# Four-chunk slabs in a LayerNorm pass, K weights loaded in pieces, and residual loads on another queue

## The reference

```python
xn = _layernorm(x)                       # mean and variance over 4096 features
qkv = einsum('bsd,od->bso', xn, w_qkv)   # 32 query heads, 8 key/value heads of 128
q, k = rope(q), rope(k)
attn = softmax(where(causal, q @ k.T / sqrt(128), min)) @ v
attn_out = einsum('bso,do->bsd', attn, w_o)
ffn_out = xn @ kernel + bias + lora_delta(xn) + shared_lora_delta(xn)
return x + attn_out + ffn_out
```

## Time and profile before

| | us |
|---|---|
| median of two timed runs | 6041.11 (5918.13 to 6164.09) |
| profiled execution, timed | 5750.58 |
| its span on the slowest core (core 7) | 5749.0 |
| spans of the other cores | 5671.9 to 5723.1 |
| PE busy / DVE / ACT / POOL on core 7 | 4163.0 / 1117.4 / 977.1 / 556.1 |

### The profile page before, as it was taken

How to read it: one execution, slowest core, us unless ns; L and a number is a source line. 1 busy time by engine, 2 the same in 40 slices (tenths; PEclk the granted TensorE clock), 3 DMA queues, 4 the chain that set the end, 5 groups by cost and what they waited for, 6 DMA issues and landing times.

```text
span 5749.0 us, 44972 instructions; the slowest of 8 cores (5671.9 to 5749.0 us)
## 1 busy us (share of the span) xinstructions
PE 4163.0 (72%) x16144; PEld 1520.2 (26%) x16144; DVE 1117.4 (19%) x1874; ACT 977.1 (17%) x1041; POOL 556.1 (10%) x866
## 2 busy tenths in 40 slices
PE   2233399769959996767777777777775999557788
PEld 0000144334424441111111111111111444223333
DVE  0444322201102221111111111111111110011122
ACT  2232000000000003333333333333332000000000
POOL 0000000000000001111111111111111000010110
PEclk9666699889979998888888888888887999778899
DMA  9666332353256650010000000000003553465543
GB/s 141 121 123 119 105 106 77 85 120 103 82 101 92 94 77 28 27 30 26 26 26 26 28 26 27 26 26 26 26 27 57 96 93 62 92 121 127 126 102 96
DMA packets 412761, 419.81 MB, mean 73 GB/s; under 512 B 63360, under 2 KB 374912, under 8 KB 412160
## 3 DMA queue, kind: packets, MB, share of 16 engines
q0 software_dynamic: 219712, 249.10, 24.6%
q1 hardware_dynamic: 192832, 167.82, 9.5%
HBM read 495.46 MB, written 83.89 MB: 101 GB/s over the span
## 4 chain that ended last, share of the span: by engine, by line
PE 64%; DMA 11%; ACT 8%; DVE 8%; another core or an unknown queue 6%; issue 3%; POOL 0%; DVEq 0%; ACTq 0%; SPq 0%; POOLq 0%
PE kv_p L86 15%; PE a_rw L81 10%; PE a_av L86 9%; ACT a_p L81 8%; PE w_p L86 8%; PE q_p L86 7%; PE f_p L86 7%; DMA sc_xkv<-lkv_o 6%; DVE a_rc L81 4%; DMA f_at<-sc_at 3%; PE a_s L86 2%; PE a_s L81 2%; DVE lkv_o L81 1%; PE f_pl L86 1%
## 5 line engine op out<-in xcount | busy, mean ns | idle before, releaser
L81 ACT ACTIVATE a_p<-a_s,p_btab 128x1024 bf16<-128x1024 f32 x768 | 814.7, 1111 | 2982.1 <-PE a_s L81 2982.0
L86 PE MATMUL a_av<-a_p,a_v 128*128 128x512 bf16 x1536 | 644.2, 419 | 417.9 <-ACT a_p L81 299.9
L81 PE MATMUL a_rw<-a_p,p_onesb 128*1 128x512 bf16 x1536 | 627.9, 409 | 0.0
L86 PE MATMUL f_p<-f_k,f_x 128*128 128x512 bf16 x2048 | 472.9, 391 | 162.4 <-DVE f_s L81 111.6
L86 PE MATMUL kv_p<-kv_w,kv_x 128*128 128x512 bf16 x1984 | 441.1, 380 | 83.3 <-DMA kv_w<-wvT 83.3
L86 PE MATMUL q_p<-q_x,q_w 128*128 128x512 bf16 x1984 | 440.6, 380 | 71.8 <-DMA q_x<-sc_xkv 71.8
L86 PE MATMUL kv_p<-kv_x,kv_w 128*128 128x512 bf16 x1984 | 440.0, 380 | 69.2 <-DMA kv_x<-sc_xkv 69.2
L86 PE MATMUL w_p<-w_w,p_attn 128*128 128x512 bf16 x1984 | 441.5, 381 | 39.1 <-DMA w_w<-woT 39.1
L81 DVE TENSOR_TENSOR a_p<-a_p,p_cm 128x512 bf16<-128x512 bf16 x256 | 97.5, 422 | 1687.2 <-ACT a_p L81 1687.2
L86 PEld LDWEIGHTS a_av<-a_p,a_v 128*128 128x128 bf16 x1536 | 148.6, 97 | 911.4 <-issue 911.4
L86 PE MATMUL a_s<-a_q,a_k 128*128 128x512 bf16 x768 | 317.3, 413 | 12.8 <-DMA a_k<-sc_k 12.8
(11 more groups left out here) (93 smaller groups left out, 2182.0 us busy)
## 6 DMA issues: line engine op xcount, KB each, us to landing
kv_x<-sc_xkv SPq DMA_DIRECT2D x16, 4096.0 KB, 17.6
lkv_x<-xTkv POOLq DMA_DIRECT2D x8, 4096.0 KB, 37.3
sc_xkv<-lkv_o SPq DMA_DIRECT2D x256, 128.0 KB, 1.9
q_w<-wqT POOLq DMA_DIRECT2D x16, 2048.0 KB, 16.4
w_w<-woT POOLq DMA_DIRECT2D x8, 4096.0 KB, 26.1
f_k<-kern POOLq DMA_DIRECT2D x8, 4096.0 KB, 26.1
a_k<-sc_k POOLq DMA_DIRECT2D x384, 64.0 KB, 2.1
a_v<-sc_v POOLq DMA_DIRECT2D x192, 128.0 KB, 2.7
```

Of the source, the lines that this page charges most:

```text
L81: getattr(eng, m)(*aa, **kk).then_inc(s, st)
L86: getattr(eng, m)(*aa, **kk)
```

## The change

Four edits. In `ln_pass` the squares, the additions and the multiplications work on slabs of four groups (128x2048) instead of single groups, and one store writes a slab (512 KB); in the statistics loop the sum matmuls of a slab are now issued after the wait for its square. The mean and reciprocal rows are given to VectorE as an operand repeated four times. The buffers `lkv_q`, `lkv_t` and `lkv_o` grow fourfold. The K weights are issued in eight pieces of 1 MB by a hook that `ln_pass` calls once in each chunk, right behind the load of the next chunk. In `final_phase` the loads of `f_xc` and `f_at` move from the `gd` queue to the `sy` queue.

```diff
--- before.py
+++ after.py
@@ -206,14 +206,15 @@
     def fview(t):
         return t.rearrange("(a p) t -> p a t", p=128)
 
-    def ln_pass(xT_in, ntok, sc_out, tag):
+    def ln_pass(xT_in, ntok, sc_out, tag, hook=None):
         nch = ntok // CH
+        SLAB = 4 * CH
         with ExitStack() as ps:
             pp = ps.enter_context
             xch = [pp(nc.sbuf_tensor(f"l{tag}_x{i}", [128, 32 * CH], BF16)) for i in range(2)]
-            sq = [pp(nc.sbuf_tensor(f"l{tag}_q{i}", [128, CH], BF16)) for i in range(2)]
-            tb = [pp(nc.sbuf_tensor(f"l{tag}_t{i}", [128, CH], BF16)) for i in range(2)]
-            ob = [pp(nc.sbuf_tensor(f"l{tag}_o{i}", [128, CH], BF16)) for i in range(2)]
+            sq = [pp(nc.sbuf_tensor(f"l{tag}_q{i}", [128, SLAB], BF16)) for i in range(2)]
+            tb = [pp(nc.sbuf_tensor(f"l{tag}_t{i}", [128, SLAB], BF16)) for i in range(2)]
+            ob = [pp(nc.sbuf_tensor(f"l{tag}_o{i}", [128, SLAB], BF16)) for i in range(2)]
             srow = pp(nc.sbuf_tensor(f"l{tag}_s", [1, CH], F32))
             qrow = pp(nc.sbuf_tensor(f"l{tag}_ss", [1, CH], F32))
             mrow = pp(nc.sbuf_tensor(f"l{tag}_m", [1, CH], F32))
@@ -232,7 +233,6 @@
             tdep = [0, 0]
             odep = [None, None]
             row_done = 0
-            pe_stats_done = 0
             gd.wait(s_ve, xfree[0])
             xload[0] = gd.dma(out=xch[0][:].rearrange("p (a t) -> p a t", a=32),
                               in_=fview(xT_in)[:, :, 0:CH])
@@ -244,19 +244,25 @@
                     xload[ni] = gd.dma(
                         out=xch[ni][:].rearrange("p (a t) -> p a t", a=32),
                         in_=fview(xT_in)[:, :, (tc + 1) * CH:(tc + 2) * CH])
+                if hook is not None:
+                    hook(tc)
                 pe.waitd(xload[xi])
                 pe.wait(s_ve, row_done)
-                for dc in range(32):
-                    si = dc % 2
-                    xt = xch[xi][:, dc * CH:(dc + 1) * CH]
-                    pe.call("matmul", p_sum[0:1, :], sb_onesb[:, 0:1], xt,
-                            start=(dc == 0), stop=(dc == 31))
+                for sl in range(8):
+                    si = sl % 2
                     ac.waitd(xload[xi])
                     ac.wait(s_pe, qdep[si])
-                    av = ac.call("activation", sq[si][:], xt, AF.Square)
+                    av = ac.call("activation", sq[si][:],
+                                 xch[xi][:, sl * SLAB:(sl + 1) * SLAB], AF.Square)
                     pe.wait(s_ac, av)
-                    pq = pe.call("matmul", p_sq[0:1, :], sb_onesb[:, 0:1], sq[si][:],
-                                 start=(dc == 0), stop=(dc == 31))
+                    for k in range(4):
+                        dc = 4 * sl + k
+                        pe.call("matmul", p_sum[0:1, :], sb_onesb[:, 0:1],
+                                xch[xi][:, dc * CH:(dc + 1) * CH],
+                                start=(dc == 0), stop=(dc == 31))
+                        pq = pe.call("matmul", p_sq[0:1, :], sb_onesb[:, 0:1],
+                                     sq[si][:, k * CH:(k + 1) * CH],
+                                     start=(dc == 0), stop=(dc == 31))
                     qdep[si] = pq
                 pe_stats_done = pe.ctr.v
                 ve.wait(s_pe, pe_stats_done)
@@ -291,21 +297,27 @@
                 ve.call("tensor_copy", bcm[:], p_bc[:, 0:CH])
                 bcv = ve.call("tensor_copy", bcr[:], p_bc[:, CH:2 * CH])
                 ve.wait(s_ve, bcv)
+                bcm_b = bcm[:].unsqueeze(1).broadcast_to((128, 4, CH))
+                bcr_b = bcr[:].unsqueeze(1).broadcast_to((128, 4, CH))
                 last_tt = 0
-                for dc in range(32):
-                    ti = dc % 2
+                for sl in range(8):
+                    ti = sl % 2
                     ve.wait(s_ve, tdep[ti])
-                    v1 = ve.call("tensor_add", tb[ti][:],
-                                 xch[xi][:, dc * CH:(dc + 1) * CH], bcm[:])
+                    xs = xch[xi][:, sl * SLAB:(sl + 1) * SLAB]
+                    v1 = ve.call("tensor_add",
+                                 tb[ti][:].rearrange("p (a t) -> p a t", a=4),
+                                 xs.rearrange("p (a t) -> p a t", a=4), bcm_b)
                     ve.waitd(odep[ti])
                     ve.wait(s_ve, v1)
-                    v2 = ve.call("tensor_mul", ob[ti][:], tb[ti][:], bcr[:])
+                    v2 = ve.call("tensor_mul",
+                                 ob[ti][:].rearrange("p (a t) -> p a t", a=4),
+                                 tb[ti][:].rearrange("p (a t) -> p a t", a=4), bcr_b)
                     tdep[ti] = v2
                     last_tt = v2
                     sy.wait(s_ve, v2)
                     odep[ti] = sy.dma(
-                        out=sc_out[dc * 128:(dc + 1) * 128, tc * CH:(tc + 1) * CH],
-                        in_=ob[ti][:])
+                        out=fview(sc_out)[:, 4 * sl:4 * sl + 4, tc * CH:(tc + 1) * CH],
+                        in_=ob[ti][:].rearrange("p (a t) -> p a t", a=4))
                 xfree[xi] = last_tt
 
     def rope_block(b0, b1, cs, sn, bufs, dst0, dst1):
@@ -430,12 +442,15 @@
         kv_sinb = plk(nc.sbuf_tensor("kv_sin", [128, S], BF16))
         wk_deps = [gd.dma(out=kv_cosb[:], in_=i_cos_kv),
                    gd.dma(out=kv_sinb[:], in_=i_sin_kv)]
-        for piece in range(4):
-            wk_deps.append(gd.dma(
-                out=wsb[:].rearrange("p (a o) -> p a o", a=32)[
-                    :, piece * 8:(piece + 1) * 8, :],
-                in_=fview(i_wkT)[:, piece * 8:(piece + 1) * 8, :]))
-        ln_pass(i_xTkv, S, sc_xkv, "kv")
+
+        def wk_hook(tc):
+            if tc < 8:
+                wk_deps.append(gd.dma(
+                    out=wsb[:].rearrange("p (a o) -> p a o", a=32)[
+                        :, tc * 4:(tc + 1) * 4, :],
+                    in_=fview(i_wkT)[:, tc * 4:(tc + 1) * 4, :]))
+
+        ln_pass(i_xTkv, S, sc_xkv, "kv", hook=wk_hook)
         barrier()
         kv_sweeps(wsb, kv_cosb, kv_sinb, wk_deps)
     barrier()
@@ -798,16 +813,16 @@
                 xcv = None
                 for tt in range(8):
                     if tt % 4 == 0:
-                        gd.wait(s_ve, xcdep)
-                        xcv = gd.dma(out=xc[:].rearrange("p (a t) -> p a t", a=4),
+                        sy.wait(s_ve, xcdep)
+                        xcv = sy.dma(out=xc[:].rearrange("p (a t) -> p a t", a=4),
                                      in_=i_xown.rearrange("(a p) d -> p a d", p=128)[
                                          :, tt // 4 * 4:tt // 4 * 4 + 4,
                                          oc * CH:(oc + 1) * CH])
                     par = tt % 2
                     pb = pf[par]
                     api = tt % 2
-                    gd.wait(s_ve, atdep[api])
-                    av_ = gd.dma(out=at[api][:],
+                    sy.wait(s_ve, atdep[api])
+                    av_ = sy.dma(out=at[api][:],
                                  in_=sc_at[tt * 128:(tt + 1) * 128,
                                            oc * CH:(oc + 1) * CH])
                     pe.waitd(kv_[ki])
```

## The result

| | before | changed |
|---|---|---|
| median of the timed runs, us | 5901.5 (10 runs) | 5479.51 (11 runs) |
| lowest, us | 5767.34 | 5456.22 |
| ratio | 1 | 0.9478, interval 0.9457 to 0.950 |

The change makes the kernel 5.2% faster; of 5768 us that is 301 us, against 296 forecast.

The account below looks back on a forecast made before the run. It saw a LayerNorm pass waiting on two chunk buffers and stores, and a last phase held by sc_at loads behind kern; 176 + 120 = 296 us off the 6041 us median gave 5745, range 5450 to 5900.

Parts of the forecast that it names:

- (a): Start of LayerNorm pass: K weights behind x let x0 land at about 62 us instead of 103, 41 us saved.
- The sum of 107 us for two chunks: LayerNorm pass, per buffer: load 41, statistics 20, rows 9.3, normalising 37 us, so 54 us a chunk.
- (b): LayerNorm statistics: eight slab squares instead of 32 take 20 us a chunk instead of 21, bounds 17 and 29.
- (c): LayerNorm normalising: 16 slab operations of at most 1.36 us, 35 to 40 us a chunk beside a load.
- The pair beside a load: LayerNorm normalising: two 512 KB stores during an x load take 8 to 16 us, 12 taken.
- Rival 1: LayerNorm pass: stores starve by turns during loads, chunk 61 us, 260 us saved in all, 5781 us; chance 0.17.
- (d): Last phase: sc_at and xown loads on the sync queue save 18.3 us in six blocks, 10 in the first, together 120.
- tile 2 is then free of the kern load: Last phase, block head: after 1 to 2 us lost at tile 1, kern no longer delays tile 2's load.
- as now: Last phase, tile 4 of a block: the xown load there was expected to behave as before the change.
- the 2.6 us and the landing: Last phase, SP's queue: 2.6 us before a tile's load is issued, plus its landing time T, against 8.2 a tile.
- the 19.9 us lost per block: Last phase before the change: block of 85.4 us less 65.5 us of matmul, laid to sc_at loads queued behind kern.
- Rival 3: Last phase, SP's queue: not faster if 2.6 us plus landing eats the 176 us gain, from 8.4 us landing; chance 0.02.

Follow-up runs that it names:

- e1: Kernel before with only the LayerNorm slabs (statistics and normalising), K weights ahead of x, last phase as before; two timed runs, 5542 and 5557 us.
- e7: Changed kernel with the statistics as before (32 squares of 512 columns); one timed run, 5479.8 us.
- e4: Changed kernel with each sc_at load issued a tile ahead, before the store of the present tile; ratio to before 0.9414, interval 0.9331 to 0.9496.
- e5: Changed kernel with four slab-sized output buffers in the LayerNorm pass instead of two; one timed run, 5437 us.

## Why the prediction was right, step by step

The total (296 forecast, 301 timed) and each of its two halves came out near: the pass 176 forecast, 176 on core 7 and 170 in the mean; the last phase 120 forecast, 95 in the mean. Inside, some steps were right for their own reasons and some only in the sum.

(a) *x0 at 62 us.* It was 54, nearer to the lower bound of 50 (6 MB at 6.9 us): x1, issued right behind, took little from x0. The saving at the start, 41 forecast, was 48. But as a part of the gain it is the step that failed: e1 has nearly the same K sweep start (474 against 470) without it. I had counted the weight piece only as a floor of the chunk (51 us) and 7 us of DMA time, and not as a price on each chunk; its measured price is 7.0 to 7.8. That the sum still fitted is luck: two errors cancelled. The sum of 107 us for two chunks holds no term for the piece, and gives the load 41 us and the normalising 37 for the slabs alone. Without the piece these two measured 35.3 and 27.4 (e1), with it 39.6 and 38.4. The slabs alone were better than forecast by about what the piece took.

(b) *Statistics 20 us a chunk.* Right in size (first square at 55.72, VectorE reads the sums at 75.79), worth nothing in the end, by e7. I had taken 1 us a chunk.

(c) *Normalising in slabs.* The rate was kept (1.23 us, forecast at most 1.36). The pair beside a load was mis-sized: 15.0 us in the mean with the pieces and 13.0 without (e1, 12 pairs), forecast 12, within the bounds of 8 and 16. (In its working, 34.6 us for the 4 MB of f_x is 8.65 us a MB and not 8.3, which changes nothing.) The load was 46 us in the first of these chunks (109.77 to 155.80) and 37 to 40 in the others, forecast 41; the chunk 54.4 (forecast 54), the K sweep 471.7 on core 7 (forecast 472). Rival 1 (starvation by turns, 61 us a chunk) is out as a forecast for these slabs. Its rule from the Trainium skill (DMA: Bandwidth & Descriptors, Queues, rings and completion order), that the DMA engines turn between queues by packets, fits the traces in so far as even the smallest pair of stores takes some 8 us. My reading of it, that a store of four times the bytes needs several such turns, is borne out in part: four times the bytes cost 1.6 to 1.7 times the time (15.0 against 9.2 us with the pieces, 13.0 against 7.7 without), neither the same nor four times.

(d) *Last phase.* The first two tiles of a block came as worked out: first addition at +16.8 us from the kern load's issue (forecast 16), second at +26.6 (forecast 26). The step that failed is "tile 2 is then free of the kern load". Its load took 6 us and not 2, for kern itself now lands after 31.3 us in the median of core 7 instead of 26.1; and at tile 4, which I had called "as now", the load of tile 5 used to be issued together with that of tile 4 and now has to wait for tile 4's store. So the 2.6 us and the landing are paid in every tile. Block 71.3 instead of 67.1: 6 x 4.2 = 25 us, which is about what is missing of the 120. It is not quite one for one: counted from the first kern load, the last phase gained 100 us in the mean (601 instead of 701), and about 5 us were lost ahead of it. e4 takes that order away and reaches 65.6. I had also read all of the 19.9 us lost per block as waiting; 2.5 of them were slower matmuls at a lower clock. Rival 3 was this same chain; its threshold was not reached, but it was at work.

The level: 5745 was forecast as the median of before less 296. The median came out at 5479.5, near the 5455 that I worked out from the profiled execution. Carrying the two long timed runs along was the wrong choice, as ten runs of before show (four of them lie between 5767 and 5785). The forecast of 5745 is 265 us too long, nearly the size of the gain; the range of 5450 to 5900 held the result only near its lower end. The gain was forecast well, the level was not.

## What to carry to other kernels

A chain of small stores through two buffers costs a round trip each. Beside a large converting load that round trip grows, but much less than the bytes of the store do: merging four stores into one cut the cost per byte to about 0.4 (13.0 us for 1 MB against 7.7 for 256 KB, or 15.0 against 9.2 with the pieces between the loads). Moving a transfer to another place of the same DMA-heavy pass won almost nothing with two buffers: what it won at the start it gave back, chunk by chunk, because it lengthened both the load and the stores on the chain of every buffer. When a load is moved to a queue that also carries the stores, ask in which order the two stand there: issue the next load before the wait of the present store. And before a full DMA busy share is taken for the limit, more buffers are worth a try (e5: 27 us off a pass with a share of 0.95).

## What I had not expected of the hardware

Beside a converting x load with a weight piece behind it, pairs of stores of 128, 256 and 512 KB each took 9.2, 10.3 and 15.0 us in the mean. Two x loads issued 2 us apart on the same queue land one after the other (first square at 55.7 us, the second chunk's at 87.5), almost without slowing the first. A 1 MB weight piece costs 7.0 to 7.8 us of a chunk that without it has a DMA share of 0.87, about what it costs at the start of the kernel, where 18 MB took 124 us (6.9 a MB). And behind a stall of 16.8 us TensorE's next 32 matmuls took 9.83 us instead of 7.08, so the stall cost more than its own length.
